# Mixing matrices split once at 128x128, loaded as high and low halves, and made ahead of the cast of x

## The reference

```
x = x + L0(x)   # att = softmax(MLP(cond)); agg_w = sum_k att[b,k] * weight[k]; agg_w[b] @ x[b] + bias
x = x + L1(x)   # grouped conv over time: 9 taps, 4 groups of 32 channels; + c @ c_weight + bias
x = x + L2(x)   # as L0, with other weights
x = x + L3(x)   # as L1, with other weights
```

## Time and profile before

| | before |
|---|---|
| time, median of 3 runs | 3067.23 us (3064.52 to 3067.24) |
| profiled execution | 3059.13 us, its span 3057.3 us |
| mean granted clock of TensorE | 0.996 of full speed |
| busy: PE, PE weight loads | 2919.7 us (95%), 2803.7 us (92%) |
| busy: DVE, POOL, ACT | 2050.8 us (67%), 1789.0 us (59%), 1458.8 us (48%) |
| DMA queue q1 | 489.46 MB, 60.8% of 16 engines' span |

### The profile page before, as it was taken

One profiled execution on the slowest core, in us unless ns is written; L12 is line 12 of the kernel. 1 busy time (PEld: TensorE's weight loads), 2 busy tenths in 40 slices (PEclk: granted clock), 3 DMA queues, 4 the chain that ended last, 5 costly groups with the idle time before them and its releaser, 6 DMA issues.

```text
span 3057.3 us, 123405 instructions
## 1 busy us (share of the span) xinstructions
PE 2919.7 (95%) x49220; PEld 2803.7 (92%) x49220; DVE 2050.8 (67%) x2587; ACT 1458.8 (48%) x2333; POOL 1789.0 (59%) x1801
## 2 busy tenths in 40 slices
PE   6999999999999999999999999999999999999998
PEld 5999999999999999999999999999999999998997
DVE  6666667666766666666666666766676666666664
ACT  4454444444454445444545444544444444544454
POOL 4565556565656565656556655665565656565653
PEclk8999999999999999999999999999999999999999
DMA  4665665566556666666666566666655665666554
GB/s 125 154 159 157 162 174 156 157 165 171 156 157 164 170 157 157 165 169 158 158 167 164 157 157 171 163 158 162 174 156 157 165 170 157 156 164 169 157 157 136
DMA packets 375112, 489.80 MB, mean 160 GB/s; under 512 B 63400, under 2 KB 227376, under 8 KB 358704
## 3 DMA queue, kind: packets, MB, share of 16 engines
q1 hardware_dynamic: 375088, 489.46, 60.8%
HBM read 205.04 MB, written 150.99 MB: 116 GB/s over the span
## 4 chain that ended last, share of the span: by engine, by line
SPq 47%; DMA 25%; DVE 16%; issue 7%; PE 3%; DVEq 1%; POOL 0%; ACT 0%; ACTq 0%
SPq L223 37%; DMA x_t<-x 24%; DVE m_sum L530 6%; SPq L178 5%; DVE prod L524 5%; DVE xp L490 5%; SPq L184 4%; PE ps L306 2%; PE ps L291 1%; SPq L221 1%; DMA m_raw<-mixed 0%; ACT x_t L456 0%; POOL xp L626 0%; DVEq L488 0%; DVEq L529 0%
## 5 line engine op out<-in xcount | busy, mean ns | idle before, releaser
L306 PE MATMUL ps<-y,conv_parts 32*128 32x512 f32 x36864 | 2743.1, 390 | 104.2 <-ACT o_ph L459 102.1
L306 PEld LDWEIGHTS ps<-y,conv_parts 32*128 32x128 f32 x36864 | 2495.4, 184 | 206.1 <-issue 154.1
L423 ACT ACTIVATE y<-ps,bias 128x512 fp32r<-128x512 f32 x1536 | 1011.5, 700 | 581.8 <-PE ps L306 548.6
L554 DVE SCALAR_TENSOR_TENSOR y<-ps,bias,y 128x512 fp32r<-128x512 f32 x1536 | 1075.4, 747 | 199.2 <-ACT y L423 195.5
L626 POOL TENSOR_TENSOR xp<-x_t,xp 128x512 fp32r<-128x512 f32 x512 | 788.7, 1573 | 9.3 <-DVE xp L490 9.3
L619 POOL TENSOR_TENSOR m_parts<-m_raw,m_parts 128x512 fp32r<-128x512 f32 x256 | 447.5, 1748 | 534.2 <-ACT m_parts L430 534.2
L490 DVE CAST xp<-x_t 128x512 fp32r<-128x512 f32 x512 | 185.5, 426 | 762.4 <-DMA x_t<-x 762.4
L291 PE MATMUL ps<-y,m_parts 32*128 32x512 f32 x6144 | 684.7, 396 | 0.0
L291 PE MATMUL ps<-xp,m_parts 32*128 32x512 f32 x6144 | 653.3, 391 | 7.3 <-issue 5.4
L430 ACT CAST m_parts<-m_raw 128x512 fp32r<-128x512 f32 x256 | 164.5, 643 | 973.3 <-DMA m_raw<-mixed 973.3
L291 PEld LDWEIGHTS ps<-xp,m_parts 32*128 32x128 f32 x6144 | 558.2, 184 | 16.3 <-issue 7.9
(11 more groups left out here) (40 smaller groups left out, 38.6 us busy)
## 6 DMA issues: line engine op xcount, KB each, us to landing
x_t<-x SPq DMA_DIRECT2D x512, 256.0 KB, 5.0
o_ch<-o_ph SPq DMA_DIRECT2D x2032, 64.0 KB, 2.0
out<-o_t SPq DMA_DIRECT2D x127, 1024.0 KB, 4.9
m_raw<-mixed SPq DMA_DIRECT2D x1024, 64.0 KB, 4.3
mixed<-m_sum SPq DMA_DIRECT2D x256, 64.0 KB, 1.6
conv_raw<-conv_w SPq DMA_DIRECT2D x2, 768.0 KB, 9.8
mix_sb<-mix_w SPq DMA_DIRECT2D x2, 576.0 KB, 9.8
out<-x_t SPq DMA_DIRECT2D x4, 256.0 KB, 4.5
```

Of the source, the lines that this page charges most:

```text
L306: ins = nc.tensor.matmul(ps[:, 4 + t, :], conv_parts[layer][rows, w, PH * q + p_in, :], src[rows, a, p_in, q:q + N], start=(k == 0), stop= ...
L423: nc.scalar.activation(dst, src, ACT.Identity, bias=bias[layer][:, k % WIDTH[layer]:k % WIDTH[layer] + 1]).then_inc(high_set[layer], 1)
L554: nc.vector.scalar_tensor_tensor(out=dst, in0=src, scalar=bias[layer][:, k % WIDTH[layer]:k % WIDTH[layer] + 1], in1=high.bitcast(fp32), o ...
```

## The change

The halves of a matrix are made on DVE, straight behind its sum and at 128x128 (`m_own`, HIGH and LOW beside each other in a row of 1 KB). The DRAM scratch doubles; the store carries both halves (128 KB), and each of the four loads brings both (128 KB each) directly to `m_parts`, whose layout becomes group, half, column. `m_raw`, `matrix_high` on ACT and `matrix_low` on POOL are gone. A load now overwrites what TensorE reads, so it waits for the four tiles of the previous element's mix (`mm`) and no longer for `m_set`. On SP, layer 2's load comes a step later in the program and ahead of layer 0's; its store moves ahead of the sixteen `o_ch` DMAs. On DVE, the two matrices of a step come ahead of the cast of x, from step 1 on. On POOL, `x_low` moves ahead of `conv_low_part(3)` in step 0. In the prologue, the softmax comes ahead of the first cast of x, and ACT's first `att_rows` ahead of the cast of conv 1's weights.

```diff
             def store_matrix(layer, j):
-                sp.wait_ge(summed[layer], j + 1)
-                sp.dma_start(scratch[layer // 2][bass.ds(j, 1)].rearrange("s c o -> (s c) o"), m_sum[layer][:]).then_inc(stored[layer], 16)
+                sp.wait_ge(own_set[layer], j + 1)
+                sp.dma_start(scratch[layer // 2][bass.ds(j, 1)].rearrange("s c w o -> (s c) (w o)"),
+                             flat(m_own[layer], "w o").bitcast(fp32)).then_inc(stored[layer], 16)
             def load_matrix(layer, j, first):
...
-                    sp.wait_ge(m_set[layer], j)
+                    sp.wait_ge(mm[layer], 4 * j)
                 for q in range(G):
-                    sp.dma_start(m_raw[layer][CG * q:CG * (q + 1)],
-                                 scratch[layer // 2][bass.ds(j, 1)].rearrange("s (g c) o -> (s c) g o", g=G)).then_inc(m_in[layer], 16)
+                    sp.dma_start(m_parts[layer][CG * q:CG * (q + 1)].rearrange("c g w o -> c g (w o)").bitcast(fp32),
+                                 scratch[layer // 2][bass.ds(j, 1)].rearrange("s (g c) w o -> (s c) g (w o)", g=G)).then_inc(m_in[layer], 16)
...
                 if t == 0 and k == 0:
-                    pe.wait_ge(m_set[layer], j + 1)
+                    pe.wait_ge(m_in[layer], 16 * G * (j + 1))
...
-                if has(i, inner, -1):
-                    matrix_high(0, i + 1, not inner and i == -1)
...
-                if now:
-                    matrix_high(2, i, not inner and i == 0)
...
+                nc.vector.tensor_reduce(m_sum[layer][:], prod[layer][:], AX_X, ALU.add).then_inc(summed[layer], 1)
+                dve.wait_ge(summed[layer], j + 1)
                 if not first:
                     dve.wait_ge(stored[layer], 16 * j)
-                nc.vector.tensor_reduce(m_sum[layer][:], prod[layer][:], AX_X, ALU.add).then_inc(summed[layer], 1)
+                nc.vector.tensor_copy(m_own[layer][:, HIGH], m_sum[layer][:]).then_inc(own_high[layer], 1)
+                dve.wait_ge(own_high[layer], j + 1)
+                nc.vector.tensor_tensor(m_own[layer][:, LOW], m_sum[layer][:], m_own[layer][:, HIGH].bitcast(fp32),
+                                        ALU.subtract).then_inc(own_set[layer], 1)
             dve.wait_ge(first_in, 32)
-            x_high(0, True)
             for l in range(2):
...
+            x_high(0, True)
             conv_identity(1)
...
-            def matrix_low(layer, j):
-                pool.wait_ge(m_high_set[layer], j + 1)
-                nc.gpsimd.tensor_tensor(m_parts[layer][:, LOW], m_raw[layer][:], m_parts[layer][:, HIGH].bitcast(fp32),
-                                        ALU.subtract).then_inc(m_set[layer], 1)
...
-                if has(i, inner, -1):
-                    matrix_low(0, i + 1)
-                if now:
-                    matrix_low(2, i)
```

More of the change, by code:

```diff
@@ L47, in build_cond_resid @@
         m_sum = {l: sb(f"m_sum{l}", [128, C]) for l in MIXES}
-        m_raw = {l: sb(f"m_raw{l}", [128, G, C]) for l in MIXES}
-        m_parts = {l: sb(f"m_parts{l}", [128, 2, G, C], f32r) for l in MIXES}
+        m_own = {l: sb(f"m_own{l}", [128, 2, C], f32r) for l in MIXES}
+        m_parts = {l: sb(f"m_parts{l}", [128, G, 2, C], f32r) for l in MIXES}
         bias = [sb(f"bias{l}", [128, WIDTH[l]]) for l in range(NL)]
@@ L115, in build_cond_resid @@
         summed = {l: sem(f"summed{l}") for l in MIXES}
+        own_high = {l: sem(f"own_high{l}") for l in MIXES}
+        own_set = {l: sem(f"own_set{l}") for l in MIXES}
         stored = {l: sem(f"stored{l}") for l in MIXES}
@@ L209, in step @@
             def step(i, inner):
+                if has(i, inner, 1) and (inner or i > 1):
+                    load_matrix(2, i - 1, False)
                 if has(i, inner, -1):
                     load_matrix(0, i + 1, not inner and i == -1)
-                if has(i, inner, 0):
-                    load_matrix(2, i, not inner and i == 0)
                 if has(i, inner, 3):
@@ L218, in step @@
                     store_matrix(0, i + 2)
+                if has(i, inner, -1):
+                    store_matrix(2, i + 1)
+                if not inner and i == -1:
+                    load_matrix(2, 0, True)
                 if has(i, inner, 2) and (inner or not is_last(i)):
@@ L290, in mix @@
                     wait_bank(t)
-                ins = nc.tensor.matmul(ps[:, t, :], m_parts[layer][rows, m, g, :], src[rows, a, g, :],
+                ins = nc.tensor.matmul(ps[:, t, :], m_parts[layer][rows, g, m, :], src[rows, a, g, :],
                                        start=(k == 0), stop=(k == MIX - 1))
@@ L399, in conv_high_part, with att_rows @@
                 nc.scalar.copy(flat(conv_parts[layer], "w s m")[:, 0:SHIFTS * 128], conv_raw[layer][:]).then_inc(conv_high_set, 1)
-            conv_high_part(1)
-            for l in range(2):
+            def att_rows(l):
                 act.wait_ge(att_mm, 2 * l + 1)
@@ L424, in high @@
                                      bias=bias[layer][:, k % WIDTH[layer]:k % WIDTH[layer] + 1]).then_inc(high_set[layer], 1)
[L426 to L430, removed]
             def step(i, inner):
@@ L564, in step @@
                         low(0, i, q, segment(LOW, q), by_phase(q), segment(HIGH, q))
-                if now and has(i, inner, -1):
+                if not inner and i == 0:
                     x_high(i + 1, False)
@@ L570, in step @@
                     matrix(2, i + 1, not inner and i == -1)
+                if now and has(i, inner, -1) and (inner or i != 0):
+                    x_high(i + 1, False)
                 if not inner and is_last(i):
@@ L642, in step @@
                     set_bias(0, i + 1)
-                if has(i, inner, -1):
-                    matrix_low(0, i + 1)
+                if now and has(i, inner, -1):
+                    x_low(i + 1)
                 if not inner and i == 0:
                     conv_low_part(3)
-                if now and has(i, inner, -1):
-                    x_low(i + 1)
                 if before and (inner or i - 1 < B):
```

10 lines of the change are left out of this document (5 added, 5 removed).

## The result

| | before | after |
|---|---|---|
| median, same chip | 3066.85 us (3064.52 to 3067.24) | 2992.03 us (2990.97 to 2993.9) |
| ratio | | 0.9758, 95% interval 0.9741 to 0.9775 |
| profiled execution, its span | 3059.13, 3057.3 us | 2990.97, 2989.2 us |
| busy PE, DVE, POOL, ACT | 2919.7, 2050.8, 1789.0, 1458.8 us | 2918.0, 2381.6, 1414.4, 1410.7 us |

The change is 75 us faster. The forecast was 25 us faster, 3042 us. The direction was right and the time lies inside the range (2962 to 3105), but the size is off by a factor of three.

A forecast was written before the change was run, and what follows sets the result against it. SP's issue ring, 23.34 us, bounds the kernel, against TensorE's own 22.31. Step 23.22 instead of 23.43 gives -26 us, prologue +1: 3059.13 - 26 + 1 = 3034, median 8.1 above: 3042 us, range 2962 to 3105.

The forecast's parts named there:

- The loss over TensorE's pace: Mean step 23.43 us against TensorE's own 22.31: 1.12 us a step, 139 us in all, the most order can give.
- the ring: From a step's start over DVE's matrices, o_ch, x's issue and layer 2's load to mix 2; step at least 23.17 us.
- the landing: From x's issue to layer 2's load being in: 8.61 us plus 0.85 for the doubled bytes, bounds 0 and 1.27.
- H: The start of ACT's first cast of a step, 1498.27 in the prediction's sample; other times are counted from it.
- my rest between instructions: On DVE, per matrix: 0.13 us for waits between dependent instructions and 0.08 for the rest.
- the port term: DVE's product delayed by POOL's copies on the shared port: 0.13 us charged, bounds 0 and 0.99.
- Rival B: The doubled load decides and the step is longer than before: 23.64 to 23.84 us, 3094 to 3119 us; chance 0.25.
- The step that failed: At mix 2: load in at H + 33.92, mix 2 begins 10.75 after a step's start, so step at least 23.17.
- R: Time from H until layer 2's load is in for the next step's mix 2; a later theory's term, mean 34.11 us.
- start-up: Prologue and first steps: softmax earlier, but x of element 1 no earlier and four matrices first; +1 us, bounds -7 and +4.
- A: Rival: landing goes by number of rows, the load is in time; -139 to -90 us, 2929 to 2978 us; chance 0.20.
- C: Rival, port lock: DVE's product waits for a whole POOL copy each step; step 24.08, +81 us, 3149 us; chance 0.05.

The follow-up runs named there:

- the last experiment: Changed kernel with layer 2's load ahead of x and x of element 1 issued right behind layer 0's first load: 2914.04 us, ratio 0.9518.
- the second experiment: Changed kernel with layer 2's load issued behind o_ch and ahead of x: 2924.76 us, ratio 0.9552 against the kernel before.
- the experiment with half the bytes: Changed kernel where all matrix loads but each layer's first bring the HIGH half alone, same number of rows: 2927.03 us, ratio 0.9558.
- the first experiment: Changed kernel with four small DMA issues added on SP between o_ch and x's issue (the added issues): 3113.82 us, ratio 1.018.

## Why the prediction was wrong in size

**What bounds the kernel before: right, and shown.** The loss over TensorE's pace, 139 us at most, is what the order of DVE alone gave back (141 us by the medians, start and end included).

**The terms of the ring: right, but for the landing.** Forecast against the mean over steps 4 to 126: both matrices done H + 13.38, measured 13.43; x issued H + 24.33, measured 24.35. The cast was put at 0.22 and took 0.23, the subtraction at 0.29 and took 0.29. In the sample a matrix takes 1503.80 - 1500.44 = 3.36 us instead of 3.47, so my rest between instructions was too high, and the port term was too low. The product over all steps (busy us, mean ns of one, idle before):

```profile
L521 DVE TENSOR_TENSOR prod<-mix_sb,att_table 128x1152 f32<-128x1152 f32 x256 | 390.1, 1524 | 0.1
```

That is 0.17 us over 1.35 for each of the two products in a step, 0.34 a step, where I charged 0.13. So the two errors nearly cancel in the mean. From x's issue to the waiting matmul I had 8.61 + 0.85 = 9.46, and it took 9.91 in the sample and 9.76 on average; the landing was under-rated by 0.30 us. Rival B's 1.27 instead of my 0.85 gives 9.88, nearer to it; its sign, a landing over 9.9 us after x's issue, is met in some steps and not in the mean (9.71).

**The step that failed: "The step is therefore at least 33.92 - 10.75 = 23.17 us".** It takes the wait at mix 2 for something that holds the same step's H. But ACT's casts at H follow work that TensorE does ahead of mix 2; the wait comes 10.97 us after H and moves only the next one. So 33.92 - 10.75 bounds no single step: the surplus of 23.17 over TensorE's 22.31, 0.86 us, is paid once in two steps. With the numbers of the prediction and half the surplus the mean is 22.31 + 0.43 = 22.74, or 124 x (22.74 - 23.43) = -86 us instead of -26. Measured in the steady state: -77; the stalls of two neighbouring steps come to 1.00 us (twice 22.81 - 22.31) instead of 0.86, half of it a step. The added issues, which made R longer by 1.92 us and the step by 0.97, show the half by themselves. That the time still fell inside the wide range is no credit to the sum: its large term, the step, was out by 51 us, and start-up, out by 8 us the other way, hid a part of that by luck.

**The second miss: start-up.** It was put at +1 us (bounds -7 and +4) and is +9.1. Step 3 starts 98.27 - 94.06 = 4.2 us later than before, and the other 4.9 us come in step 3 itself, which takes 125.51 - 98.27 = 27.24 us where it took 22.31. For the first part, the causes that the prediction named were there and too cheap: x of element 1 is issued at 35.91 instead of 32.52, behind layer 2's first load, and matrices stand ahead of `low`. DVE in step 0:

```profile
43.51 3.63 DVE L487 CAST xp<-x_t 128x512 fp32r<-128x512 f32 x4 [8.36 <-DMA x_t<-x]
47.06 2.44 DVE L521 TENSOR_TENSOR prod<-mix_sb,att_table 128x1152 f32<-128x1152 f32 x1
...
50.92 3.21 DVE L529 CAST m_own<-m_sum 128x128 fp32r<-128x128 f32 x1
...
57.62 5.35 DVE L556 SCALAR_TENSOR_TENSOR y<-ps,bias,y 128x512 fp32r<-128x512 f32 x8
```

And before:

```profile
44.59 4.49 DVE L524 TENSOR_TENSOR prod<-mix_sb,att_table 128x1152 f32<-128x1152 f32 x1
...
52.80 5.83 DVE L554 SCALAR_TENSOR_TENSOR y<-ps,bias,y 128x512 fp32r<-128x512 f32 x8 [2.33 <-ACT y L423]
```

The second `low` begins at 57.62, before at 52.80, and everything behind it on TensorE follows. The product and the cast that stand beside POOL's work are 1.1 and 3.0 us longer than alone, which the prediction did not count; but before, a product in the same place was 3.1 us longer than alone, so only about 1 us of that is new. Issuing x of element 1 ten us earlier gave 10 us back at step 3's start (the last experiment against the second), with the long product and the long cast still in their places. The late x thus more than covers the 4.2 us.

The prediction had nothing for step 3. There mix 2 waits for its load, and TensorE's granted clock is at half of full speed (1.2 instead of 2.4 GHz) from 112.88 to 116.29, right behind the wait; a matmul takes 0.62 us in that stretch and 0.39 in the steady steps:

```profile
112.51 0.49 PE L294 MATMUL ps<-y,m_parts 32*128 32x512 f32 x1 [3.12 <-DMA m_parts<-mixed]
```

With layer 2's load ahead of x (the second experiment) this wait is gone, the clock stays full and step 3 takes 22.31 us: it is the load and not x of element 1 that costs these 4.9 us. The granted clock is at half in one longer stretch as well, from 51.44 to 68.50; TensorE stood still ahead of it from 49.31 to 50.68, and in it from 55.57 to 61.14, and was busy for the other 11.5 us. Before, it was at half from 39.83 to 46.65 and from 70.55 to 73.96. How much of the 4.2 us is due to the clock and how much to x was not separated.

**The sum, with what was measured:** -76.8 in the steady state, +9.1 at the start, -0.4 at the end: -68.1, and the two profiled executions differ by 68.2. The medians differ by more, 74.8, since before's profiled execution lay 7.7 us below the median of these runs and after's 1.1 below.

**The rivals.** A came nearest in size (-139 to -90 us against -77) with the wrong reason: the bytes do decide (the experiment with half the bytes), and the load is late. B was nearer on the landing, and priced it by the same wrong rule, at twice its cost. C did not come about as a whole copy each step: the mean product is 0.17 us longer than one that runs alone, and in the sample it is POOL's copies that take 1.1 us more (5.05 against 3.96 in the earlier trace rows).

The Trainium skill (SBUF — State Buffer, "SBUF: two separate sides") says that whichever of the two starts first holds the shared pair for the whole instruction and the other blocks. The trace agrees in one part: DVE's product starts at 1500.44 and takes its usual 1.36 us, and POOL's last copy, begun at 1500.60, takes 2.16 us where the other three take 1.12 each. In another it does not: the third copy had begun at 1499.64 and ran to 1500.76, and the product did not wait for it, as far as spans on POOL can be trusted.

**Left open.** How the 0.34 us of the products are shared out over the steps was not tried; they do not drive the stalls' going up and down, which is stronger in the first experiment (-0.87), where the products are hardly longer than alone. Why a stalled step comes out 0.12 us longer than its wait was not followed up. Nor were the smaller parts of start-up's 9.1 us tried one by one.

## What to carry to other kernels

Where a late arrival holds up a pipeline, count over how many steps the ring closes before you turn its lateness into a step's length: a wait that comes after the event which starts the ring is paid by the step after it, and the surplus is divided. A dummy delay on the ring shows the divisor in one run, if you read from its trace how much longer the ring really became. Where a page's chain leaves out an engine that your ring needs, check in the rows which wait ended last. And when a change has several parts, try the cheapest by itself: two lines of one engine's order carried all the gain, and the load into the single buffer that TensorE reads from cost next to nothing as soon as it landed some 1.3 us earlier, be it by its place in the queue, by an earlier issue or by fewer bytes.

## What the runs showed of the hardware

Two things were unexpected. A load of 512 KB, as four DMAs into 32 partitions each, cost by its bytes, although it had the same number of rows as one of 256 KB: from x's issue to its last landing it took 9.71 us on average, and 8.34 with 256 KB. The Trainium skill's limit of about 218 GB/s for 32 partitions (SBUF — State Buffer, "Door 1: The DMA port swizzle") would make 1.2 us of the 256 KB between the two, as an estimate; the measured 1.37 us, 191 GB/s, stays under that limit.

And DVE's cast of 128 columns, 0.23 us in every step of the sample, took 3.21 us where POOL's subtraction over 1536 columns ran beside it (`conv_parts`, from 50.59 for 3.46 us). The cast ended at 54.13, the subtraction at 54.05. The product beside POOL's subtraction of x at 47.06 took 2.44 instead of 1.35. So here a cast of DVE's waited for an instruction of POOL's that had begun 0.33 us before it, to its end. The Trainium skill (SBUF — State Buffer, "Who interferes with whom") lists casts among what can take the port pair that VectorE and GpSimd share, and says that issue order decides who blocks; these rows agree.
